# A graph network's edge layer: one [128 x 128] product for each group, or both groups in quarters of the array with VectorE's adds moved ahead

## The reference

```python
h = jnp.maximum(_layernorm(x, axis=-1), 0.0)
y = h
for l in range(5):
    hh = _leaky(y @ W1[l] + b1[l]) @ W2[l] + b2[l]               # nodes, 64 -> 128 -> 64
    e = _leaky(edge_attr @ We1[l] + be1[l]) @ We2[l] + be2[l]    # edges, 32 -> 64 -> 64
    msg = hh[src] * e * dot_scale[l]
    agg = jax.ops.segment_sum(msg, dst, num_segments=n)
    out = y + agg * res_w[l]
    y = layernorm(out) * ln_g[l] + ln_b[l]
x = x + y
```

## Time and profile before

| | |
|---|---|
| time, median of 3 runs | 6618.61 us (6609.32 to 6630.04) |
| profiled execution | 6615.82 us, its span 6614.0 us |
| busy share of the span | PE 85%, PEld 56%, DVE 78%, ACT 17%, POOL 68% |
| granted clock of TensorE, mean | 0.88 of 2.4 GHz |
| five layers begin at about | 1229, 2322, 3412, 4497 and 5588 us |
| costliest groups of instructions | POOL L793 3674.3 us; PE L980 1307.0 us; DVE L1670 of the slots 588.9 and 588.6 us |

### The profile page before, as it was taken

How to read it: one execution, slowest core, us unless ns; L and a number is a source line. 1 busy time by engine, 2 the same in 40 slices (tenths; PEclk the granted TensorE clock), 3 DMA queues, 4 the chain that set the end, 5 groups by cost and what they waited for, 6 DMA issues and landing times.

```text
span 6614.0 us, 169076 instructions
## 1 busy us (share of the span) xinstructions
PE 5622.6 (85%) x63332; PEld 3676.7 (56%) x63333; DVE 5148.4 (78%) x7991; ACT 1133.9 (17%) x1726; POOL 4527.2 (68%) x4793
## 2 busy tenths in 40 slices
PE   6776899988888788888878888888898887888887
PEld 2223444456666555666655666655566665556665
DVE  8997544688887688888768888867888875888886
ACT  0000211111122211112211112221111222111111
POOL 5777777666677377777727777746777773777775
PEclk9997555799999799999979999988999997999998
DMA  3112399755566355656635655644565563666664
GB/s 135 26 26 47 78 240 242 185 131 138 138 148 152 96 132 136 142 141 154 159 80 133 145 143 143 162 112 116 129 147 142 148 161 78 139 147 156 151 171 110
DMA packets 733545, 886.20 MB, mean 134 GB/s; under 512 B 325488, under 2 KB 502976, under 8 KB 731568
## 3 DMA queue, kind: packets, MB, share of 16 engines
q1 hardware_dynamic: 568480, 703.64, 40.8%
q0 software_dynamic: 152144, 154.93, 12.4%
q10 hardware_dynamic: 12096, 16.53, 0.8%
HBM read 749.51 MB, written 125.06 MB: 132 GB/s over the span
## 4 chain that ended last, share of the span: by engine, by line
PE 54%; DVE 21%; issue 15%; DVEq 4%; ACT 3%; DMA 1%; POOL 0%; ACTq 0%; SPq 0%; POOLq 0%
PE bank L980 14%; PE bank L976 8%; PE bank L1029 7%; PE bank L1053 5%; PE bank L922 4%; PE bank L879 3%; DVE arena L1662 3%; PE bank L1016 3%; PE bank L860 2%; PE bank L845 2%; DVEq L1782 2%; DVE arena L1750 2%; ACT arena L1241 2%; DVE arena L1670 2%; DVE arena L1408 2%
## 5 line engine op out<-in xcount | busy, mean ns | idle before, releaser
L793 POOL DMA_INDIRECT arena<-h_rows,src x3855 | 3674.3, 953 | 1693.5 <-issue 1250.7
L980 PEld LDWEIGHTS bank<-w2s,arena 128*128 128x128 f32 x8960 | 1175.7, 210 | 772.3 <-DVE arena L1750 437.2
L980 PE MATMUL bank<-w2s,arena 128*128 128x128 f32 x8960 | 1307.0, 303 | 208.2 <-DVE arena L1750 191.4
L780 POOL DMA_INDIRECT slots<-arena,slot_index x792 | 787.2, 994 | 267.2 <-issue 241.3
L976 PE MATMUL bank<-nodes_state,edge_w 64*128 64x512 f32 x980 | 598.4, 693 | 307.3 <-DVE nodes_state L1718 142.6
L1053 PEld LDWEIGHTS bank<-arena 112*64 112x64 f32 x20160 | 640.4, 138 | 267.0 <-issue 245.1
L1053 PE MATMUL bank<-arena 112*64 112x64 f32 x20160 | 725.8, 225 | 60.1 <-issue 54.2
L976 PE MATMUL bank<-x_packed,edge_w 64*128 64x512 f32 x1260 | 740.1, 669 | 16.4 <-ACT std L1190 15.6
L1241 ACT ACTIVATE arena<-bank,tenth 128x512 f32<-128x512 f32 x490 | 335.5, 685 | 2296.6 <-PE bank L976 2296.6
L1662 DVE SCALAR_TENSOR_TENSOR arena<-bank,edge_w,arena 128x512 f32<-128x512 f32 x490 | 366.7, 748 | 424.1 <-ACT arena L1241 421.4
L1670 DVE TENSOR_TENSOR x_packed<-bank,slot_rel 128x2880 f32<-128x2880 f32 (+8 forms) x315 | 588.9, 1870 | 15.8 <-issue 15.8
(11 more groups left out here) (198 smaller groups left out, 5615.6 us busy)
## 6 DMA issues: line engine op xcount, KB each, us to landing
arena<-slot_pick SPq DMA_DIRECT2D x630, 448.0 KB
arena<-h_rows SPq DMA_DIRECT2D x630, 224.0 KB
x_packed<-slot_attr SPq DMA_DIRECT2D x630, 128.0 KB
nodes_state<-attr_t SPq DMA_DIRECT2D x485, 128.0 KB
arena<-h_rows,src POOLq DMA_INDIRECT x3855
slot_pick<-arena SPq DMA_DIRECT2D x126, 448.0 KB
x_packed<-slots SPq DMA_DIRECT2D x127, 136.0 KB, 4.9
slots<-arena SPq DMA_DIRECT2D x9, 1904.0 KB, 22.1
```

Source lines behind the costliest of these rows:

```text
L780: pool.indirect_dma_start(slots, bass.IndirectOffsetOnAxis(ap=slot_index[:, t:t + 1], axis=0), records[:, v, j, :], None).then_inc(record_ ...
L793: pool.indirect_dma_start(to[0:n, at:at + D], None, table, bass.IndirectOffsetOnAxis(ap=index[0:n, t:t + 1], axis=0)).then_inc(landed(t), 16)
L980: mm = pe.matmul(to[:, j * P:(j + 1) * P], acts[:, j * TILE:(j + 1) * TILE], w2s[:, :], start=True, stop=True)
```

## The change

1. Where both a gathered and a slot group are due, their second products are made together by `edge_out_both`, 32 matmuls of 64 rows and 64 columns with 64 columns moving, in place of 8 of 128 by 128. Upper rows feed one bank and lower rows the other, then the two change places, and between these halves PE waits for its own matmuls (`halves_out`). The empty quarters of `w2s` are no longer multiplied. Both waits, for `msg_ready` and for `slot_msg_ready`, come ahead of it. A step with one of the groups alone keeps `edge_out`.
2. Each product raises its semaphore by 2.
3. On DVE the register loads of the window and the two L1718 come right after the L1666, ahead of the tile parts "middle" and of the slot group's one-hot matrix.

```diff
+            def edge_out_both(acts, slot_acts, pairs):
+                own_wait(pe, "pe")
+                for side in range(2):
+                    for j in range(TPH):
+                        for half in range(2):
+                            edges_of = slice(j * TILE + half * D, j * TILE + (half + 1) * D)
+                            outs = slice(half * D, (half + 1) * D)
+                            for k, to, of in ((side, e_ps, acts), (1 - side, slot_ps, slot_acts)):
+                                at, rows_of = (2 * j + k) * D, slice(k * D, (k + 1) * D)
+                                mm = pe.matmul(to[outs, at:at + D], of[rows_of, edges_of], w2s[rows_of, rows_of],
+                                               start=True, stop=True)
+                                if j == TPH - 1:
+                                    done = halves_out if side == 0 else e_ready if of is acts else slot_e_ready
+                                    mm.then_inc(done, 1)
+                    if side == 0:
+                        pe.wait_ge(halves_out, 4 * pairs)
+                        own_wait(pe, "pe")
...
+                    if b_at(s) is not None:
+                        pe.wait_ge(slot_msg_ready, l * NB + s + 1)
+                    k = b_at(s + 1)
                     if m is not None:
                         pe.wait_ge(hid_acted[0], l * GA + m + 1)
-                        edge_out(hidden[:, 0, m % 2, :], e_ps).then_inc(e_ready, 1)
-                    k = b_at(s)
-                    if k is not None:
-                        pe.wait_ge(slot_msg_ready, l * NB + k + 1)
-                    k = b_at(s + 1)
                     if k is not None:
                         pe.wait_ge(hid_acted[1], l * NB + k + 1)
-                        edge_out(hidden[:, 1, k % 2, :], slot_ps).then_inc(slot_e_ready, 1)
+                    if m is not None and k is not None:
+                        edge_out_both(hidden[:, 0, m % 2, :], hidden[:, 1, k % 2, :], l * PAIRS + pairs_before(s) + 1)
+                    elif m is not None:
+                        edge_out(hidden[:, 0, m % 2, :], e_ps).then_inc(e_ready, 2)
+                    elif k is not None:
+                        edge_out(hidden[:, 1, k % 2, :], slot_ps).then_inc(slot_e_ready, 2)
...
                     if m is not None:
-                        dve.wait_ge(e_ready, l * GA + m + 1)
+                        dve.wait_ge(e_ready, 2 * (l * GA + m + 1))
                         edge_biased(e_ps[:, :], e_ps[:, :]).then_inc(e_biased, 1)
+                    if k is not None and k != SPILL_AT:
+                        group = GB0 + real(k)
+                        window_start[:] = [dve.value_load(start_i[0:1, 2 * group + side:2 * group + side + 1],
+                                                          min_val=0, max_val=NPAD) for side in range(2)]
+                        window_added(s, k)
                     part("middle")
...
-                    if k is not None and k != SPILL_AT:
-                        group = GB0 + real(k)
-                        window_start[:] = [dve.value_load(start_i[0:1, 2 * group + side:2 * group + side + 1],
-                                                          min_val=0, max_val=NPAD) for side in range(2)]
-                        window_added(s, k)
                     if ends_chunk(s):
                         chunk_added(s)
```

More of the change, by code:

```diff
@@ L124, in windows_before, with pairs_before @@
         return 2 * (k - (k > SPILL_AT))
+    def pairs_before(s):
+        return sum(1 for j in range(-1, s) if a_at(j + 1) is not None and b_at(j + 1) is not None)
+    PAIRS = pairs_before(STEPS)
     def adds_before(s):
@@ L337, in build @@
         msg_ready, slot_msg_ready = sem("msg_ready"), sem("slot_msg_ready")
+        halves_out = sem("halves_out")
         win_ready, sum_ready, added = sem("win_ready"), sem("sum_ready"), sem("added")
```

2 lines of the change are left out of this document (1 added, 1 removed).

## The result

The changed kernel takes 6760.67 us (median of 4 runs, 6740.74 to 6789.11) where the kernel before takes 6619.20 beside it: a ratio of 1.0215, 95% interval 1.0179 to 1.0252. It is 2.1% slower. The prediction was 6566 us, a little faster, with a range that ended at 6700: wrong in its sign, and the time lies outside its range.

What follows compares the result with a forecast made beforehand. No engine was full; DVE (820 us) and PE (863 us) bound each layer's 980 us of slot steps, POOL third. Terms -5 - 10 - 8 + 7.5 + 5 = -10.5 us a layer, -52 over five: 6618.6 to 6566 us, range 6440 to 6700.

Steps and rivals of the forecast that it cites:

- gap now: Steps whose own group is missing: gain 0.80 us in wide chunks, 0.6 in middle, 0.3 in narrow; 19 us a layer.
- gap next: Steps where the group of the next step is missing: cost 0.12 us, 34 times, 4 us a layer.
- gap after: Steps where the group of step s+2 is missing: cost 0.35 us, 34 times, 12 us a layer.
- full: The 24 steps a layer with groups for s, s+1 and s+2: gain 0.1 us each, 2 us a layer.
- Part 2: L1718 and its loads ahead of the slot one-hot on DVE: ordinary steps gain 5 us a layer.
- the tile parts: Twelve tiles a layer: bare loads at sub-step 0 cost 7.5 us, an earlier chain at sub-step 1 gains 8 us.
- Part 1: Pair in quarters on PE: 1.5 us instead of 2.05, ready at +2.93 us of a step; gains 10 us a layer.
- Clock: PE's clock in the slot steps: 16 us a layer more at the lower level, 5 us of it felt.
- the pair isn't shorter: Rival: pair takes 2.4 us, ready at +3.83; 73 us a layer lost, and the 10 us gain too; 6980 us, chance 0.08.
- The rival that the clock falls: Time at 1.2 GHz on PE doubles, 20 us felt instead of 5; layer loses 11 us: 6676 us, chance 0.17.
- Nothing measurable: Rival: DVE's bare register loads give back all that the freed L976 gains; 6618 us, chance 0.20.
- The gathers' reserve of about 70 us: POOL's gathers end some 70 us ahead, so a layer can shrink by about 70 us before they bind.

Runs made afterwards that it cites:

- i3: Kernel before, with all waits of the pair ahead of both full-size calls and DVE's new order (the changed kernel without quarters): 6743.72 us, ratio 1.0197.
- b_order: Kernel before, with only DVE's order changed: register loads and the two L1718 ahead of tile parts and slot one-hot; single calls kept: 6545.24 us, ratio 0.9884.
- f3_loads: b_order with the window's two register loads issued right after L1757, ahead of the waits for the pair: 6479.8 us, ratio 0.9794.
- c_joint: Kernel before, with only the waits for both messages and both activations moved ahead of both calls; products stay 128 x 128: 6753.45 us, ratio 1.0199.
- j2: Changed kernel, with the window's two register loads issued right behind the second L1757 product, ahead of the waits for the pair: 6660.61 us, ratio 1.0082.
- k2: i3 with the window's two register loads issued early, ahead of the waits for the pair; full-size products: 6631.60 us, ratio 1.0037.
- a_quarters: Changed kernel with the loads and the two L1718 back behind the one-hot matrix, so quarters and joint waits alone: 6763.06 us, ratio 1.0207.

## Why the prediction was wrong

The mean length of a step by kind, worked out from the starts of L1757 in all five layers (w, m, n: first, middle and last third of a layer's steps; "tile": steps in which a tile is taken along; i3 is i3_joint_order; "chunk ends": eight of the nine steps a layer that end a chunk, which are in their own rows too), shows each term at its place:

```
kind, steps              before  b_order  f3_loads  c_joint   i3    after    j2     k2
gap now, w     30         8.38     7.79     7.81     8.34    7.90    7.82    7.90   7.90
gap now, m     20         7.45     6.60     6.78     7.50    6.70    6.77    6.86   6.94
gap now, n     20         5.82     5.57     5.69     5.83    5.63    5.85    5.87   5.69
gap next, w    30         7.47     7.60     6.95     7.50    7.49    7.62    7.11   6.89
gap after, w   30         7.73     8.13     7.75     8.42    8.83    9.16    8.54   8.53
gap after, n   20         5.55     5.95     5.53     6.25    6.57    7.23    6.54   5.96
full, w        30         8.00     8.00     7.97     8.29    8.58    8.52    8.18   8.19
tile, m       135         8.74     8.42     8.45     9.01    8.82    8.74    8.59   8.78
tile, n       135         7.59     7.52     7.48     7.78    7.79    7.91    7.84   7.72
chunk ends     40        10.21     9.15     8.92    10.46    9.60    9.54    9.28   9.37
```

**Part 2 was right in direction, and too small in the sum.** Its terms for a single step were near: gap now gains 0.80, 0.6 and 0.3 us, gap next costs 0.12, gap after next costs 0.35, a full step gains 0.1. b_order measured 0.59, 0.85 and 0.25; 0.13; 0.40; 0.00. But b_order's slot steps are 14.4 us a layer shorter (74 us in all are 15), where 5.5 were forecast. Taken over all steps, tile steps among them, and with the chunk ends apart, a layer changes like this:

```
us a layer              gap now  gap next  gap after  full   chunk ends
forecast                 -19       +4        +12       -2     none
b_order less before      -18.1     -0.6      +6.8      +6.0   -8.5
```

The four kinds together came near their forecast of -5 (-5.9, with the tile parts, forecast at -0.5, among them). What is missing is the chunk ends, to which the prediction gave no term, though it read L1731's 1.31 us of idle in the earlier trace rows as the price of two loads: the new order puts the one-hot matrix ahead of L1731 and covers that idle, 38 us over the span (42.9 to 4.7). It gave none either to L1718 waiting for PE's window sums, 1.6 us before and 111.9 in b_order, which the shorter waits before L1662 and L1666 more than paid.

**Part 1 is the step that failed.** "The pair is ready at 1.40 + 1.5 + 0.03 = +2.93", and "so where DVE leads the step, part 1 gives nothing", and 10 us a layer elsewhere: with its clock cost, part 1 was to gain 5 us a layer. Alone, in a_quarters, it lost 144 us, 29 a layer. In the step shown the pair starts 0.22 us later than the first term has it, and from the first matmul to L1693 are 1.74 us instead of 1.53: ready at +3.36, late by 0.43. Over all pairs the median from L1784's start to the pair's end is 2.74 us, where the prediction has 2.33. The wait between the halves, taken as 0.1 us without a row for it, was 0.32 in the mean (146.5 us in 459 waits over the span). The pace itself, 21 ns a record from the earlier trace rows, was right: a half is 0.69 us. The Trainium skill ("TensorE: Matmul & The Clock Gate", section "Wait — 56ns, not 53.3ns?") has about 25 ns as the least from start to start. The records of the pair don't agree: 0.69 us for 32, and from the first start to the last 0.48 us (median), 15 ns a record. The 1.7 us to which that figure led was as near to the 1.62 measured as my 1.5, but only by the wait in the middle.

**The first mistake in it is to price the pair by its length, though DVE waits for its end.** The quarters save 0.43 us of length, and the joint wait puts the start 0.82 us later. c_joint shows the latter alone: with nothing shortened, the wait before L1666 rises by 116 us over the span, and the kernel by 2.0%. The 0.4 us that quarters save on top gains nothing that can be told (1.0207 against 1.0199).

**The second is that the parts were summed.** That L1718 finds DVE "free at +4.46" and so its loads covered in a full step needed the pair at +2.93. With single calls it is so (full, w: 8.00 in b_order); with the late pair the loads begin later and lie bare: a full step of the changed kernel is 0.52 us longer than before, and one with the gap after next 1.43 (+0.35 forecast), of which c_joint has 0.69 and b_order 0.40. In this last kind the two simply add up (i3 has 1.10), and the other 0.33 come with the quarters; in the full step they don't (0.29 and 0.00 alone, 0.58 together). In f3, j2 and k2 the loads are taken out of the comparison: there the joint wait costs 2.4% by itself.

**Clock.** 5 us a layer were forecast, for a clock a little lower because PE stands longer before L1757. The granted clock over each layer's slot steps (first to last L1757), and its mean:

```
layer             0      1      2      3      4     mean
before           0.95   0.95   0.96   0.95   0.95   0.954
b_order          0.96   0.96   0.97   0.97   0.96   0.963
c_joint          0.95   0.95   0.95   0.95   0.95   0.948
i3_joint_order   0.95   0.96   0.96   0.95   0.95   0.953
k2_joint_loads   0.95   0.95   0.95   0.95   0.96   0.954
a_quarters       0.92   0.92   0.92   0.91   0.92   0.919
after            0.92   0.92   0.94   0.92   0.91   0.921
j2_after_loads   0.93   0.93   0.94   0.94   0.92   0.931
```

So the clock falls with the quarters, not with the joint wait. Worked out from the means, some 90 us of a layer's slot steps ran at 1.2 GHz before, 105 in c_joint (the forecast had 16 more) and 160 in the change. PE is busy 39 us a layer less than before, where 50 were forecast. The lower clock falls on pairs too: from a pair's first start to its last, 69 of 460 pairs before and 88 of 460 in c_joint took over 2.15 us where 1.78 is usual, and 207 of 912 halves of quarters took over 0.6 where 0.48 is usual. It is the likely reason that quarters gain nothing over full-size products with the same waits, but what it costs by itself wasn't measured.

**The rivals.** The nearest in time is the one that I gave 0.08: "the pair isn't shorter", ready 0.9 us late, 83 us a layer, deciding "from a pair of 1.7 us on". The pair is shorter, but ready 0.43 us later than assumed, half of that. b_order to the change is 215 us, 43 a layer, half of 83. Its arithmetic was sound; its cause, and so its chance, was read from the pair's length only. The rival that the clock falls had 0.17 for a doubled time at 1.2 GHz, and 90 us became 160: its condition nearly came true, and the sign named for it, a granted clock under 0.94 in the slot steps, is met by the mean of 0.921. But its 6676 us is not what happened, since c_joint loses 2.0% with the clock almost as before. "Nothing measurable" assumed that the bare loads give back the gain: with the joint wait they do (c_joint to i3: 0.02 points).

## What to carry to other kernels

When an edit merges two products so that they must wait for both inputs, price the moment at which the result is ready, not the time that the engine is busy: moving a start behind one more product of 0.6 us cost more than the array's better use could return. Sum two edits only if neither uses the other's slack, and give register loads that a moved instruction needs their cover first (issued ahead of the next wait, that gave 0.9 to 1.6% here). When two edits come together, run each alone: here one was a gain of 1.2%, hidden under the other's loss.

## What the runs showed of the hardware

- PE waiting for its own matmuls before it goes on costs 0.32 us in the mean (459 waits, 146.5 us) and 0.26 in the median, while the records before it are only 0.69 us long.
- 64 records of 64 x 64 quarters take 1.62 us with that wait, the same work in 64-row by 128-column products 2.47, and at 128 x 128 with twice the multiplications 2.05.
- The order of waits ahead of a product has a price: when the one that is met last stood last, a second wait instruction followed in PE's queue, the start came 0.15 us later (median), and the kernel took 70 us more.
- Quarters leave TensorE less busy and the granted clock lower: 0.92 in the slot steps (a_quarters, the change), where full-size products with the same joint wait have 0.95 (c_joint, i3_joint_order).
- The gathers' reserve of about 70 us was there in four layers, but not in the last: from the last gather to the last L1750 are 72 us in the earlier trace rows, and 36 in the last layer of the kernel before. In f3_loads, whose slot steps are 23 to 32 us a layer shorter, they are 58 to 60 us in the three middle layers and 8 in the last, where three of the last products with gathered rows wait for gathers (10.4 of 11.8 us in 4 waits).
